# Multi-head attention with residual on one core: transposes by halves between the projections, relu on ScalarE, Pool's adds one step later

## What is computed

```python
q = _split_heads(jnp.einsum('bfe,ed->bfd', x, W_query))
k = _split_heads(jnp.einsum('bfe,ed->bfd', x, W_key))
v = _split_heads(jnp.einsum('bfe,ed->bfd', x, W_value))
scores = jnp.einsum('hbqd,hbkd->hbqk', q, k)
attn = jax.nn.softmax(scores, axis=-1)
out = jnp.einsum('hbqk,hbkd->hbqd', attn, v)
out = out.transpose(1, 2, 0, 3).reshape(x.shape[0], x.shape[1], HEADS * ATT_D)
out = out + jnp.einsum('bfe,ed->bfd', x, W_res)
return jax.nn.relu(out)
```

## Time and profile before

| what | value |
|---|---|
| median of 3 runs | 1569.93 us |
| time of the profiled execution | 1570.47 us |
| its span, first to last instruction | 1568.7 us |
| mean granted TensorE clock | 0.998 |
| ACT busy | 1094.8 us (70%) |
| POOL busy | 1270.0 us (81%) |
| HBM traffic | 86 GB/s over the span |

### The profile page before, as it was taken

The page is one execution under the profiler, slowest core; times in us unless marked ns, Lnnn a source line. Parts: engine busy times, 40 slices in busy tenths (PEclk is TensorE's granted clock), DMA queues, the critical chain, the costliest instruction groups (busy, mean ns, idle before and its releaser), DMA issues.

```text
span 1568.7 us, 77760 instructions
## 1 busy us (share of the span) xinstructions
PE 1546.8 (99%) x32768; PEld 1416.5 (90%) x32768; DVE 1392.5 (89%) x1793; ACT 1094.8 (70%) x1794; POOL 1270.0 (81%) x1804
## 2 busy tenths in 40 slices
PE   7999999999999999999999999999999999999997
PEld 6999999999999999999999999999999999999996
DVE  6989898989898989899989898989898989898995
ACT  4777777777777777777777777767676767676765
POOL 4888888888888888888888888888888888888887
PEclk9999999999999999999999999999999999999999
DMA  3444444444444444444444444444444444444442
GB/s 65 92 86 89 86 88 87 88 87 88 88 87 87 88 87 87 87 87 87 87 87 87 88 87 87 87 88 87 87 88 87 88 87 88 88 87 88 87 89 61
DMA packets 677306, 135.40 MB, mean 86 GB/s; under 512 B 545888, under 2 KB 677216, under 8 KB 677216
## 3 DMA queue, kind: packets, MB, share of 16 engines
q1 hardware_dynamic: 675840, 134.30, 41.5%
q10 hardware_dynamic: 1376, 0.26, 0.1%
HBM read 67.37 MB, written 67.11 MB: 86 GB/s over the span
## 4 chain that ended last, share of the span: by engine, by line
PE 98%; POOL 1%; issue 0%; DVE 0%; DMA 0%; ACTq 0%; ACT 0%; POOLq 0%
PE ps_so L243 18%; PE ps_pt L234 17%; PE ps_so L223 14%; PE ps_qk L199 12%; PE ps_qk L200 8%; PE ps_vr L212 8%; PE ps_qk L201 8%; PE ps_vr L213 8%; PE ps_vr L214 8%; POOL y L155 0%; POOL y L161 0%; DMA w_raw<-in_L_rec_W_res_dram 0%; ACTq L332 0%; POOL v_diag L170 0%; POOLq L40 0%
## 5 line engine op out<-in xcount | busy, mean ns | idle before, releaser
L155 POOL TENSOR_TENSOR y<-attn,vr 128x256 f32<-128x256 f32 x512 | 386.1, 774 | 168.9 <-POOL v_diag L170 164.5
L170 POOL COPY v_diag<-vr 64x264 f32<-64x264 f32 x1024 | 415.8, 406 | 103.9 <-POOL y L161 40.6
L307 ACT COPY probs_t<-ps_pt 128x512 f32<-128x512 f32 x512 | 274.9, 589 | 306.2 <-PE ps_pt L234 306.2
L161 POOL TENSOR_SCALAR y<-y 128x512 f32<-128x512 f32 x256 | 462.0, 1805 | 22.4
L362 DVE TENSOR_REDUCE row_max<-ps_so 128x16 f32<-128x1024 f32 x256 | 313.5, 1225 | 122.0 <-PE ps_so L223 122.0
L292 ACT COPY qk<-ps_qk 128x512 f32<-128x512 f32 x512 | 300.7, 587 | 118.9 <-PE ps_qk L201 98.9
L199 PE MATMUL ps_qk<-x_hi,w_hi 128*128 128x256 f32 x1024 | 338.0, 330 | 11.0 <-DVE x_lo L353 9.8
L299 ACT COPY vr<-ps_vr 128x512 f32<-128x512 f32 x512 | 298.9, 584 | 32.9
L367 DVE TENSOR_TENSOR shifted<-ps_so,row_max 128x1024 f32<-128x1024 f32 x256 | 313.5, 1225 | 8.8
L243 PE MATMUL ps_so<-v_diag,probs_t 128*64 128x66 f32 x8192 | 296.4, 224 | 2.8 <-POOL v_diag L170 2.5
L212 PE MATMUL ps_vr<-w_hi,x_hi 128*128 128x256 f32 x1024 | 290.0, 283 | 0.7 <-ACT vr L299 0.7
(11 more groups left out here) (21 smaller groups left out, 1702.5 us busy)
## 6 DMA issues: line engine op xcount, KB each, us to landing
x_in<-in_r_x_dram SPq DMA_DIRECT2D x1024, 64.0 KB, 2.2
out_dram<-y SPq DMA_DIRECT2D x256, 256.0 KB, 2.3
w_raw<-in_L_rec_W_query_dram ACTq DMA_DIRECT2D x1, 64.0 KB, 2.4
w_raw<-in_L_rec_W_key_dram ACTq DMA_DIRECT2D x1, 64.0 KB, 2.6
w_raw<-in_L_rec_W_value_dram ACTq DMA_DIRECT2D x2, 32.0 KB, 2.7
w_raw<-in_L_rec_W_res_dram ACTq DMA_DIRECT2D x2, 32.0 KB, 2.7
```

Of the source, the lines that this page charges most:

```text
L155: nc.gpsimd.tensor_tensor(y[:, n % 2, a * HALF:(a + 1) * HALF].rearrange("k t (p j d) -> k j (t p) d", j=2, d=D), attn[:, n % 2, a * HALF: ...
L161: nc.gpsimd.tensor_scalar(y[:, n % 2], y[:, n % 2], 0.0, None, ALU.max).then_inc(y_ready, 1)
L170: nc.gpsimd.tensor_copy(v_diag[n % 2][j * F:(j + 1) * F, seq, :, :, :, j].rearrange("k a t p d -> k a (t p) d"), vr[n][seq * F:(seq + 1) * ...
```

## The change

1. `ps_pt` gets one bank instead of two. Both halves of the transposes write the same bank, and the transposes of half 1 wait until ScalarE has copied half 0 out.
2. TensorE's order within a step becomes: transposes half 0, `project_qk` half 0, `project_vr` half 0, transposes half 1, `project_qk` half 1, `project_vr` half 1. ScalarE's copies follow the same order: `copy_pt(i-1, 1)` moves behind `copy_vr(i, 0)`.
3. The relu leaves Pool. ScalarE does it in place on `y` of body i-4 as its first instruction of step i (`clip`), and that sets `y_ready`.
4. Pool's two adds in step i are for body i-3 (before: i-2). They wait for the store of body i-5, which used the same buffer of `y`. The copies of v no longer wait for the relu, only for the adds of the same step.
5. SyncE stores body i-4 in step i (before: i-2), and the loops run to N + 4 steps (before: N + 2).

```diff
-        ps_qk, ps_vr, ps_pt = banks("ps_qk"), banks("ps_vr"), banks("ps_pt", 2)
+        ps_qk, ps_vr, ps_pt = banks("ps_qk"), banks("ps_vr"), banks("ps_pt")
...
-                if has(i - 2):
-                    sp.wait_ge(y_ready, i - 1)
-                    sp.dma_start(out_bodies[i - 2], y[:, n % 2]).then_inc(y_stored[n % 2], 16)
+                if has(i - 4):
+                    sp.wait_ge(y_ready, i - 3)
+                    sp.dma_start(out_bodies[i - 4], y[:, n % 2]).then_inc(y_stored[n % 2], 16)
...
-                if has(i - 2):
-                    pool.wait_ge(attn_ready, i - 1)
-                    if has(i - 4):
-                        pool.wait_ge(y_stored[n % 2], dma_count(i - 4, n, 1))
+                if has(i - 3):
+                    pool.wait_ge(attn_ready, i - 2)
+                    if has(i - 5):
+                        pool.wait_ge(y_stored[(n + 1) % 2], dma_count(i - 5, n + 1, 1))
...
-                    pool.wait_ge(sum_ready, halves(i - 2, 1))
-                    nc.gpsimd.tensor_scalar(y[:, n % 2], y[:, n % 2], 0.0, None, ALU.max).then_inc(y_ready, 1)
...
-                    if has(i - 2):
-                        pool.wait_ge(y_ready, i - 1)
+                    if has(i - 3):
+                        pool.wait_ge(sum_ready, halves(i - 3, 1))
...
             def transpose_probs(i, a):
-                if has(i - 1):
-                    pe.wait_ge(pt_ready, halves(i - 1, a))
+                if a == 1 or has(i - 1):
+                    pe.wait_ge(pt_ready, halves(i, a) - 1)
...
                 if has(i - 1):
                     pe.wait_ge(probs_ready, i)
                     transpose_probs(i - 1, 0)
-                    transpose_probs(i - 1, 1)
                 if has(i + 1):
                     project_qk(i + 1, (n + 1) % RING, 0)
                 if has(i):
                     project_vr(i, n, 0)
+                if has(i - 1):
+                    transpose_probs(i - 1, 1)
...
+            def clip(i, n):
+                act.wait_ge(sum_ready, halves(i, 1))
+                nc.scalar.activation(y[:, n].rearrange("k t c -> k (t c)"), y[:, n].rearrange("k t c -> k (t c)"),
+                                     ACT.Relu).then_inc(y_ready, 1)
...
             def step(i, n):
+                if has(i - 4):
+                    clip(i - 4, n % 2)
                 if has(i - 1):
                     copy_pt(i - 1, 0)
-                    copy_pt(i - 1, 1)
                 if has(i + 1):
                     copy_qk(i + 1, 0)
                 if has(i):
                     copy_vr(i, n, 0)
+                if has(i - 1):
+                    copy_pt(i - 1, 1)
```

More of the change, by code:

```diff
@@ L98, in run @@
         def run(step):
-            for i in range(N + 2):
+            for i in range(N + 4):
                 step(i, i % RING)
@@ L149, in step @@
             def step(i, n):
-                if has(i - 2):
-                    pool.wait_ge(attn_ready, i - 1)
-                    if has(i - 4):
-                        pool.wait_ge(y_stored[n % 2], dma_count(i - 4, n, 1))
+                if has(i - 3):
+                    pool.wait_ge(attn_ready, i - 2)
+                    if has(i - 5):
+                        pool.wait_ge(y_stored[(n + 1) % 2], dma_count(i - 5, n + 1, 1))
                     for a in range(2):
                         nc.gpsimd.tensor_tensor(
-                            y[:, n % 2, a * HALF:(a + 1) * HALF].rearrange("k t (p j d) -> k j (t p) d", j=2, d=D),
-                            attn[:, n % 2, a * HALF:(a + 1) * HALF].rearrange("k t (p j) d -> k j (t p) d", j=2),
-                            vr[(n + 2) % RING][:, a, 2:4, :, :, 0:D].rearrange("k j t p d -> k j (t p) d"),
+                            y[:, (n + 1) % 2, a * HALF:(a + 1) * HALF].rearrange("k t (p j d) -> k j (t p) d", j=2, d=D),
+                            attn[:, (n + 1) % 2, a * HALF:(a + 1) * HALF].rearrange("k t (p j) d -> k j (t p) d", j=2),
+                            vr[(n + 1) % RING][:, a, 2:4, :, :, 0:D].rearrange("k j t p d -> k j (t p) d"),
                             ALU.add).then_inc(sum_ready, 1)
-                    pool.wait_ge(sum_ready, halves(i - 2, 1))
-                    nc.gpsimd.tensor_scalar(y[:, n % 2], y[:, n % 2], 0.0, None, ALU.max).then_inc(y_ready, 1)
                 if has(i):
@@ L233, in transpose_probs @@
                         c, pair = t * PAIRS + p, probs[:, a * HALF + t, p * 2:p * 2 + 2, :].rearrange("q j f -> q (j f)")
-                        last = nc.tensor.transpose(ps_pt[:, a * BANK + c * P:a * BANK + (c + 1) * P], pair, ident[:, :])
+                        last = nc.tensor.transpose(ps_pt[:, c * P:(c + 1) * P], pair, ident[:, :])
                 last.then_inc(pt_done, 1)
@@ L306, in copy_pt @@
                     act.wait_ge(o_done, i)
-                nc.scalar.copy(probs_t[:, a].rearrange("p c q -> p (c q)"), ps_pt[:, a * BANK:(a + 1) * BANK]).then_inc(pt_ready, 1)
+                nc.scalar.copy(probs_t[:, a].rearrange("p c q -> p (c q)"), ps_pt[:, :]).then_inc(pt_ready, 1)
             def step(i, n):
+                if has(i - 4):
+                    clip(i - 4, n % 2)
                 if has(i - 1):
                     copy_pt(i - 1, 0)
-                    copy_pt(i - 1, 1)
                 if has(i + 1):
```

## The result

The changed kernel takes **1513.87 us** (median of 4 runs, 1513.70 to 1514.19) against 1569.99 us for the kernel before beside it: ratio 0.9643, 95% interval 0.9626 to 0.9660. Forecast were 1513.3 us.

A forecast was written before the change was run, and what follows sets the result against it. The prediction took TensorE's steady step of 6.03 us, with 0.22 us lost waiting for ScalarE's copy of `ps_qk`, as the bound. 248 x 0.22 = 54.6 us plus 2 at the end gave 1513.3 us, range 1502 to 1542.

The forecast's parts named there:

- The sum: Whole kernel: 54.6 us from the steady steps and 2 us at the end, 1570.47 - 56.6 = 1513.9 profiled, 1513.3 as median.
- The stall: TensorE before `project_qk` half 1: weight load waits for ScalarE's copy of `ps_qk`; 0.22 us lost a step, 248 steps.
- The end of the span: Last body's relu, 1.48 us on Pool, becomes 0.6 on ScalarE; -2 us taken (-3 to 0).
- served in bunches: ScalarE's queue: the copy of `ps_qk` was said to run late behind two copies of transposed probabilities, 804.57 to 805.64.
- the walk: One new step timed instruction by instruction from its first transpose as zero; claimed the step goes from 6.03 to 5.81 us.
- The new switch: TensorE, from `project_vr` half 0 to transposes half 1: claimed to cost 0, range to 0.15 us.
- Rival (a): TensorE's added change from projection to transpose costs up to 0.15 us x 254 = 38 us, up to 1551; chance 0.18.
- the cover before the next `copy_pt`: ScalarE, from the relu's end at 6.15 to the next step's `copy_pt` half 0 at 6.51: 0.35 us claimed.
- The two covers at TensorE: Spare time at `project_qk` half 1 (0.3 us, 0.2 for the weight load) and at `project_vr` half 1 (0.3 us).
- Rival (b): ScalarE turns late elsewhere, `copy_pt` half 0 slipping; 1568 if all 0.22 us came back; chance 0.10 together with (d).
- (d): TensorE's wait only moves to `project_vr` half 1, 0.3 us of cover: 1513 to 1568; chance 0.10 together with Rival (b).
- rival c: ScalarE: relu and exp evict each other's table, 1.28 us a load; 1910 us and over, 1590 with one a step; chance 0.04.

## Why the prediction was right, and where it was not

**The sum** held term by term. The stall: 248 x 0.22 = 54.6 us; the waits are gone, and the step went from 6.03 to 5.81. The end of the span: from the last reduce of the scores (1551.70 before, 1496.75 after) to the end of the span it took 17.0 us and takes 15.2: -1.8 us where -2 stood. The two parts run alone show the split: with the order alone the end still takes 17.0 us, with relu, Pool and SyncE alone it takes 15.2, so the 1.8 us belong to the relu and Pool, and everything in the steady step to the order. The round through the single `ps_pt` bank that the prediction added at the end cost nothing that these times show.

**The cause named for the stall was wrong.** "ScalarE is not short of time; it is served in bunches" failed: the run with ScalarE's order alone didn't move. The number that spoke against it was in the rows of before: the six matmuls of `ps_qk` half 0 start up to 805.40, and a record lasts 0.28, so they are complete at 805.68; `copy_qk` starts at 805.72, not held up by the copies ahead of it. I had compared the copy's start with the matmul's start. The forecast came out right since the walk itself used the right times (matmul end, copy, signal) and what moved in between the halves was the cover needed. The number was not luck, but the named cause would have misled whoever acted on it: it promised up to the whole gain for ScalarE's order alone, which gives nothing.

**The new switch** from projection to transpose: 0 was taken of 0 to 0.15, from the row nearest in shape, and 0.12 us to the first transpose, the plain pace, show 0. Rival (a) is out. The Trainium skill's sentence that a weight load overlaps matmuls in flight only for other rows of the array ("TensorE: Matmul & The Clock Gate", "Part 3: Packing small matmuls") disagrees with both switches: full 128*128 tiles follow full 128*128 tiles with new weights and no gap. The same section names a background weight buffer as a second case in which a load goes ahead; these rows are at least not against that.

**ScalarE**: relu 0.64 us where 0.6 was taken; the cover before the next `copy_pt` was forecast too small, 0.35 us where 0.68 us are idle, because instructions in a row start 0.48 us apart and not 0.59. The two covers at TensorE (0.2 to 0.3 us) were right for `project_qk`: 0.22 by experiment. The one for `project_vr` was not tried by itself. Rival (b) is out, and so is (d): TensorE's weight load at L210 waits for ScalarE's `vr` once in the whole span, 0.3 us, and the step is the forecast one.

**The table** (rival c): the changed kernel's trace holds one table load of 1283 ns, as before, with 256 relus between 256 exps. The Trainium skill's statement that relu stands in every table set ("ScalarE: Activation LUTs", "Table sets: the hidden batching unit") agrees.

**Pool, SyncE, VectorE**: the adds start 2.94 us after the first transpose (807.71 - 804.77), 2.6 was forecast; the store lands after 2.5 us instead of 2.3. It costs nothing, as the run of the order alone, without this wait, has the same step. `x_lo` fell to 0.70 us on average (0.69 forecast) and bought nothing, since VectorE was never waited for.

## What to carry to other kernels

When an engine waits for the copy out of a single PSUM bank, add up the round trip (end of the last matmul, signal, copy, signal) and compare it with the work that stands between. What is missing can come from work already in the program: 0.2 us of it did here what reordering ScalarE's copies could not. Before blaming the copying engine's queue, check whether its input was complete: compare its start with the end of the matmul's record, not with the start. And a weight load goes ahead of its matmul when it may, so the cover must be larger than the idle time shows (0.12 us idle, 0.22 us lost). Read such a loss from the distance between steps: a late weight load of 0.1 us left no row in the view of the waits.

## What was not expected of the hardware

- Copies of 512 elements from PSUM on ScalarE last 0.59 us each in the record, but follow each other every 0.48 us (801.09 to 801.57); the sum of their record lengths overstates the time they take by a fifth.
- The recorded starts of small tiled matmuls don't show their pace: 32 scores have starts within 0.27 us, and the next group's first start comes after 0.41 us, after 64 in a row at 0.84.
- A projection behind scores costs 0.06 us a step more than a transpose behind scores; behind each other, projections and transposes cost nothing extra (0.12 us to the first transpose, 0.55 us for four transposes and a projection).
